# An attention and feed-forward kernel: GpSimd's last block of W_out goes to the second iteration, half of P's low part to GpSimd earlier, its square roots one step later

## What is computed

```python
query = _layernorm(x) @ w_q.T                # 32 heads of 32, in 8 groups of 4
key, value = ctx @ w_k.T, ctx @ w_v.T        # one head of 32 for each group
scores = where(mask, query . key / sqrt(32), lowest)
attention = softmax(scores)
x = x + (attention @ value) @ w_out.T
x1, x2 = split(_layernorm(x) @ w12.T + b12)
x = x + (silu(x1) * x2) @ w3.T + b3
```

## Time and profile before

| | |
|---|---|
| median of three runs | 1118.41 us |
| profiled execution: device time | 1119.04 us |
| profiled execution: span of the instructions | 1117.3 us |
| TensorE busy | 1079.1 us (97%) |
| VectorE / ScalarE / GpSimd busy | 571.1 / 425.3 / 392.8 us |
| mean granted TensorE clock | 0.987 |

### The profile page before, as it was taken

One profiled execution on the slowest core, in us unless ns is written; L12 is line 12 of the kernel. 1 busy time (PEld: TensorE's weight loads), 2 busy tenths in 40 slices (PEclk: granted clock), 3 DMA queues, 4 the chain that ended last, 5 costly groups with the idle time before them and its releaser, 6 DMA issues.

```text
span 1117.3 us, 19426 instructions
## 1 busy us (share of the span) xinstructions
PE 1079.1 (97%) x7952; PEld 658.4 (59%) x7952; DVE 571.1 (51%) x1062; ACT 425.3 (38%) x899; POOL 392.8 (35%) x376
## 2 busy tenths in 40 slices
PE   8887999999999989999999999999999999999998
PEld 7776766767768667676655544444444444444443
DVE  6869776776776766577755322631134111431121
ACT  6757555555656455455566520111110111011100
POOL 2769801613315224157686688112000300121000
PEclk8999899999999999999999999999999999999999
DMA  9657597996988858569793644370006300360001
GB/s 367 213 145 169 134 255 191 204 230 165 251 195 213 208 173 210 121 172 232 183 243 81 175 160 159 71 241 1 1 4 151 147 1 1 76 188 1 1 1 76
DMA packets 201512, 162.24 MB, mean 145 GB/s; under 512 B 162640, under 2 KB 172880, under 8 KB 196560
## 3 DMA queue, kind: packets, MB, share of 16 engines
q1 hardware_dynamic: 201424, 161.01, 54.3%
HBM read 93.87 MB, written 27.26 MB: 108 GB/s over the span
## 4 chain that ended last, share of the span: by engine, by line
PE 75%; DVE 11%; ACT 4%; DMA 2%; issue 1%; POOL 1%; SPq 0%; DVEq 0%; ACTq 0%
PE bank_dense L984 69%; ACT arena_attn L816 2%; DVE arena_in L1356 2%; DMA arena_attn<-arena_attn 2%; PE bank_score L1045 1%; PE bank_score L1041 1%; DVE arena_rows L1328 1%; DVE arena_in L1359 1%; DVE arena_in L1269 1%; DVE arena_rows L1317 1%; PE bank_dense L1001 1%; PE bank_av L1063 1%; PE bank_av L1067 1%; DVE arena_in L1373 1%; PE bank_av L1065 1%
## 5 line engine op out<-in xcount | busy, mean ns | idle before, releaser
L984 PE MATMUL bank_dense<-arena_rows,arena_in 128*128 128x256 f16 (+1 forms) x2304 | 348.1, 309 | 3.6 <-DVE small L1231 1.4
L984 PEld LDWEIGHTS bank_dense<-arena_rows,arena_in 128*128 128x128 f16 x2304 | 224.3, 98 | 111.3 <-DVE small L1231 1.7
L816 ACT ACTIVATE arena_attn<-bank_score,arena_in 128x128 f32<-128x128 f32 x512 | 192.9, 467 | 160.6 <-DVE arena_in L1359 160.6
L984 PE MATMUL bank_dense<-arena_out,arena_attn 128*128 128x512 f16 x768 | 170.5, 379 | 0.0
L984 PE MATMUL bank_dense<-arena_out,arena_in 128*128 128x512 f16 x768 | 166.1, 379 | 0.9 <-issue 0.9
L984 PE MATMUL bank_dense<-arena_attn,arena_rows 128*128 128x512 f16 x768 | 166.4, 379 | 0.0
L1408 DVE SCALAR_TENSOR_TENSOR arena_attn<-bank_dense,small,arena_attn 128x512 f32<-128x512 f32 x32 | 24.0, 751 | 221.3 <-PE bank_dense L984 221.3
L702 POOL TENSOR_TENSOR arena_attn<-arena_attn 128x512 f16<-128x512 f32 x53 | 62.6, 1181 | 199.3 <-ACT arena_attn L825 199.3
L984 PEld LDWEIGHTS bank_dense<-arena_out,arena_in 128*128 128x128 f16 x768 | 75.1, 98 | 91.7 <-issue 1.5
L984 PEld LDWEIGHTS bank_dense<-arena_attn,arena_rows 128*128 128x128 f16 x768 | 75.1, 98 | 90.6
L658 POOL TENSOR_TENSOR small<-small 128x1 f32<-128x1 f32 x32 | 24.1, 755 | 289.7 <-DVE small L1311 289.6
(11 more groups left out here) (124 smaller groups left out, 1326.1 us busy)
## 6 DMA issues: line engine op xcount, KB each, us to landing
arena_rows<-x SPq DMA_DIRECT2D x32, 512.0 KB, 6.0
arena_attn<-q_scratch SPq DMA_DIRECT2D x48, 256.0 KB, 4.6
arena_rows<-w_t SPq DMA_DIRECT2D x12, 1024.0 KB, 6.1
arena_rows<-ctx_t SPq DMA_DIRECT2D x8, 1024.0 KB, 5.9
q_scratch<-arena_attn SPq DMA_DIRECT2D x16, 512.0 KB, 5.2
x_scratch<-arena_rows SPq DMA_DIRECT2D x16, 512.0 KB, 3.9
arena_out<-x_scratch SPq DMA_DIRECT2D x16, 512.0 KB, 6.0
out<-arena_out SPq DMA_DIRECT2D x16, 512.0 KB, 3.8
```

Source lines behind the costliest of these rows:

```text
L816: ins = act.activation(e[:, g % 2, u, SEQ * j:SEQ * j + SEQ], B_SCORE[g % 2][:, SEQ * h:SEQ * h + SEQ], ACT.Exp, bias=neg_max[:, g % 2, h: ...
L984: ins = pe.matmul(dst, lhs(a, c), rhs(b, c), start=(c == 0 and n == 0), stop=(c == KC - 1 and n == 2))
```

## The change

Three things are moved; no arithmetic is added or left out.

- `PLO_ALONE` goes from 11 to 6: for groups 6 to 10 too, GpSimd does the half u = 1 of P's low part and VectorE only the half u = 0.
- GpSimd splits the three blocks of W_out in the steps listed in `WO_AT`. The first two blocks stay in steps (1, 2) to (1, 5). The third (block 1 of W_out) goes from steps (1, 6) and (1, 7) to steps (2, 1) and (2, 2), behind the context's halves.
- The roots of tiles 2t + 2 and 2t + 3, t < 7, go from steps 2 and 3 to steps 3 and 4.

```diff
-PLO_ALONE = 11
+PLO_ALONE = 6
...
+WO_AT = ((1, 2), (1, 3), (1, 4), (1, 5), (2, 1), (2, 2))
...
                         prob_lo(GROUPS * (t - 1) + s - 1)
                     if t < NB and s in (0, 1):
                         split_ctx(t, halves[s])
-                    if t == 1 and s >= 2:
-                        split_wo(s // 2 - 1, WO_ORDER[s // 2 - 1], halves[s % 2])
-                    if t < NB - 1 and s in (2, 3):
-                        root(2 * t + s)
+                    if (t, s) in WO_AT:
+                        n = WO_AT.index((t, s))
+                        split_wo(n // 2, WO_ORDER[n // 2], halves[n % 2])
+                    if t < NB - 1 and s in (3, 4):
+                        root(2 * t + s - 1)
```

## The result

Over 11 runs of each, the changed kernel takes 1125.68 us (1123.10 to 1129.92) and the kernel before 1117.77 us (1109.40 to 1119.38). The medians lie 7.9 us apart. The ratio is 1.0084, with a 95% interval of 1.0064 to 1.0104: slower by 7 to 12 us. A second comparison, beside other kernels, gave 1.0088 (1.0057 to 1.0120). The forecast was +10.0 us and 1128.4 us, with a range of 1123.5 to 1133.0.

A forecast was written before the change was run, and what follows sets the result against it. TensorE, busy 1079.1 of 1117.3 us, was taken to bound the kernel. A projection start 7.5 us later plus 2.5 us of low clock gave +10.0 us, 1128.4 us against the median of 1118.41; range 1123.5 to 1133.0 us.

The forecast's parts named there:

- The queue of GpSimd: Iteration 2: W_out's pieces queue behind context and low parts, so the first output projection starts at 155.5 us, +7.5 us.
- The shift of iteration 1: Everything from 125 us on was to come 2.5 us earlier, with 1 and 6 us as ends.
- The lock: VectorE and GpSimd share a port pair; three meetings at about 0.9 us each would end the block at 156.3 us.
- the five reliefs of 0.53 us: VectorE's operations on P's low part, groups 6 to 10: each shrinks from 1.21 to 0.68 us, 2.65 us in all.
- The low clock: Behind TensorE's wait at the first output projection: lower clock costs 2.5 us, bounds 0 and 3.4.
- The sum: Whole kernel: 7.5 us later projection plus 2.5 us of clock, +10.0 us, with nothing given back behind step (2, 3).
- the signs by which the prediction would have been wrong: Wait under 3 us, shift at 125 us over 6 us, or iterations from 3 on differing by over 1 us each.
- What came along at nothing: Later transposes of P, SyncE's queue, exponentials and roots: covered by the wait or without effect, zero.
- The relief: End of iteration 1: TensorE's 1.79 us wait for VectorE goes, up to 1.6 us of clock returns; shift 2.5 us.
- Faster: Rival: all twelve W_out pieces ready before TensorE at 145.5 us, only the relief left, 1115.4 us; 5%.
- Slower, but less: Rival: short pieces, projection starts at 152.0 us, clock stays, 1122.5 us, or 1124.2 with one short dip; 17%.
- slower, and more: Rival: long pieces and a long clock dip, 11.4 + 3.4 = 14.8 us, 1133.2 us; 16%.

The follow-up runs named there:

- the second trace: The changed kernel unaltered, run and traced once more beside other kernels, against the kernel before: ratio 1.0088 (1.0057 to 1.0120).
- wo_roots: Changed kernel with PLO_ALONE back at 11, W_out's last block in iteration 2 and later roots kept: ratio to the kernel before 1.0015 (0.9996 to 1.0034).
- wo_alone: Kernel before with only W_out's last block moved to steps (2, 1) and (2, 2): ratio 1.0027 (1.0005 to 1.0050).
- clock_kept: Changed kernel with 80 idle transposes on TensorE ahead of its wait for W_out: ratio to the kernel before 1.0072 (1.0044 to 1.0100).
- wo_first: Changed kernel with W_out's last block in steps (2, 0) and (2, 1), ahead of the context's halves: ratio to the kernel before 1.0053 (1.0022 to 1.0084).
- roots_alone: Kernel before with only the roots one step later: ratio 1.0006 (0.9988 to 1.0024).
- plo_alone: Kernel before with only the threshold of P's low part at 6: ratio 1.0007 (0.9985 to 1.0030).
- half_later: Changed kernel with the first half of W_out's last block back in (1, 6), the second in (2, 1): ratio to the kernel before 1.0010 (0.9993 to 1.0027).
- half_roots: Changed kernel with PLO_ALONE back at 11 and W_out's last block in (1, 6) and (2, 1): ratio to the kernel before 0.9999 (0.9989 to 1.0010).
- wo_back: Changed kernel with W_out's last block back in (1, 6) and (1, 7): ratio to the kernel before 0.9972 (0.9957 to 0.9986), repeated 0.9991 (0.9978 to 1.0003).

## Why the prediction was right

**The queue of GpSimd: right, nearly to the microsecond.** Every step of the sum has its row in the first trace. The shift of iteration 1 was taken as 2.5 us; the high part of group 8 was ready at 131.94 + 1.12 = 133.06 us (forecast 133.0). GpSimd idled 1.61 us ahead of its low part (1.6). The four pieces behind it ran from 134.25 to the start of the next low part, 147.13 us: 12.9 us (13.4). The last two took 154.60 - 148.24 = 6.4 us (6.7). TensorE came at 154.71 - 9.22 = 145.49 us (145.5) and started at 154.71 us (155.5). The price of 3.35 us for a piece, from the context pieces of the same iteration, was the right row to choose; they came to 3.2 us. The 3.75 us of iteration 1 would have put the start near 158 us.

**The lock: it sets single pieces, not the sum.** VectorE's timeline:

```profile
114.52 0.23 DVE L1362 TENSOR_SCALAR arena_in<-arena_in 128x8 f32<-128x8 f32 x1
...
115.58 0.67 DVE L1368 TENSOR_TENSOR arena_attn<-arena_attn 128x512 f16<-128x512 f32 x1
...
128.28 1.54 DVE L1368 TENSOR_TENSOR arena_attn<-arena_attn 128x512 f16<-128x512 f32 x1
...
135.23 0.68 DVE L1368 TENSOR_TENSOR arena_attn<-arena_attn 128x512 f16<-128x512 f32 x1
...
151.12 0.68 DVE L1368 TENSOR_TENSOR arena_attn<-arena_attn 128x512 f16<-128x512 f32 x1
```

The small scaling of the earlier trace rows that took 1.09 us takes 0.23 at 114.52 us, now that no split runs beside it, as forecast; the half low part takes 0.67 us at 115.58 us. But the half at 128.28 us took 1.54 us: GpSimd's scaling of 128.23 to 129.27 us began 0.05 us before it. So one of the five reliefs of 0.53 us was no relief. That fits the exclusive lock on the shared port pair (the Trainium skill, SBUF — State Buffer, Reading the diagram under SBUF: two separate sides), in the direction against VectorE. The end of 156.3 us that the prediction drew from the rule was too late, but not for the number of meetings: there were three. The price of 0.9 us came from a meeting with a whole low part of 1.22 us, while VectorE now has halves of 0.68 us. GpSimd's rounding at 135.36 us, begun 0.13 us into the half of 135.23 us, took 1.03 us in place of the 0.61 us of the rounding at 138.80 us; its rounding at 141.89 us took 1.02 us, and its scaling at 151.26 us, 0.14 us into the half of 151.12 us, took 1.44 us in place of 1.04. That is 0.4 us each, and 153.6 + 1.2 = 154.8 us, against 154.60 measured.

**The low clock: right in kind, 0.3 us off in the first trace and 0.9 in the second.** Windows of 2 us over the wait and the projection:

```profile
148.00:150.00 2.00, 0.00 (x0) 0.00 (x0) 1.93 (x6) 0.00 (x0) 1.89 (x3) 1.00 0.23 46
150.00:152.00 2.00, 0.00 (x0) 0.00 (x0) 1.77 (x3) 0.76 (x3) 1.89 (x2) 0.53 1.15 212
152.00:154.00 2.00, 0.00 (x0) 0.00 (x0) 0.00 (x0) 0.75 (x3) 1.86 (x3) 0.50 0.02 4
154.00:156.00 2.00, 1.29 (x4) 0.49 (x5) 0.00 (x0) 0.00 (x0) 2.00 (x3) 0.50 0.00 0
156.00:158.00 2.00, 2.00 (x6) 0.68 (x5) 0.00 (x0) 0.00 (x0) 0.22 (x1) 0.50 0.55 107
158.00:160.00 2.00, 2.00 (x6) 0.73 (x5) 0.00 (x0) 0.00 (x0) 0.00 (x0) 0.50 1.29 209
160.00:162.00 2.00, 2.00 (x9) 0.83 (x8) 0.00 (x0) 0.00 (x0) 0.00 (x0) 0.91 0.80 307
162.00:164.00 2.00, 2.00 (x17) 1.55 (x16) 1.06 (x3) 0.92 (x3) 0.00 (x0) 1.00 1.01 418
```

TensorE is idle in 148 to 154 us and its clock falls within 150 to 152 us; it is at 0.50 until about 160 us. The projection lost 8.12 - 5.35 = 2.8 us (forecast 2.5, bounds 0 and 3.4). In the second trace it lost 1.6 us, and the windows say why. There the clock was at 0.84 in 146 to 148 us, at 0.50 up to 156 us, at 0.60 in 156 to 158 us and at 1.00 from then on. So it fell near 147.4 us, 2.4 us after TensorE stopped, and was back near 157.6 us, 3.3 us into the projection. In the first trace it fell near 150.1 us, 4.6 us after TensorE stopped, and was back near 160.4 us, 5.7 us into the projection. The projection lost half of those stretches at the lower clock: 1.6 of 3.3 us and 2.8 of 5.7 us. Behind a wait of 2.74 us (wo_roots) the projection lost nothing, and behind 3.49 us (wo_alone) 1.4 us. That idling is the cause is shown by clock_kept, in its trace.

**The sum.** In the profiled executions: the stretch grew by 44.03 - 32.55 = 11.5 us, what lies ahead of it shrank by 2.0 us, and what lies behind it, 1117.3 - 157.47 = 959.8 us, took 1128.1 - 166.99 = 961.1 us. That is 11.5 - 2.0 + 1.3 = 10.8 us, against a forecast of 10.0. In the second trace it is 10.4 - 2.4 - 0.7 = 7.2 us. Over all runs it is 0.84%, 9.4 us, with 7.9 us between the medians. So the forecast lies within what the runs spread over; that one trace came within a microsecond of it is in part luck.

Behind the second projection nothing came back, as forecast. The 1.3 us there aren't explained: in the second trace the rest took 1124.5 - 165.40 = 959.1 us, 0.7 us less than before. They arise late. From the second projection to the start of a high part in the last iteration (566.70 us before, 575.50 and 573.84 us in the changed kernel) it is 409.2, 408.5 and 408.4 us, so iterations 3 to 7 as a whole are no longer than before. None of the signs by which the prediction would have been wrong came: the wait is not under 3 us, the shift not over 6, and the later iterations are not each over 1 us longer or shorter.

**What came along at nothing.** The waits of P's transposes in iteration 2 were covered, as forecast, and wo_first shows what they cost when they aren't: 3.96 us. In iteration 3 TensorE waits for a transpose, 1.61 us up to 227.89 us in the first trace and 1.95 us in the second, where the trace of before has no such wait. It isn't of one part of the change: roots_alone, plo_alone and wo_alone have one of 1.8 to 2.0 us there, and wo_roots, half_later and clock_kept have none. The roots cost and gained nothing (roots_alone).

**The relief: a right size by a split that doesn't hold.** The shift at the end of iteration 1 was 2.0 us in one trace and 2.4 in the other, against 2.5 forecast. The forecast hangs on this term one for one, since the start of the projection follows from the high part of group 8. But where the shift comes from differs between the two traces. In the first, the wait of 1.79 us for VectorE shrank to 0.15 us, yet the value projection started only 0.5 us earlier, at 118.72 us; the rest is its length of 2.79 us in place of 4.27. In the second the wait was still 1.52 us, the value projection started 2.6 us earlier, at 116.58 us, and took 4.46 us: the clock fell there again. The prediction had the wait go, for a start 1.2 to 2.2 us earlier, and up to 1.6 us of clock besides; neither trace shows both. wo_alone, without the earlier halves, has the wait of 1.62 us and a shift of 3.3 us. And half_roots, which has a shift of 3.7 us in its trace and no wait for W_out, shows no gain over its runs. That the term came out near 2.5 us is luck as far as these runs tell.

**The rivals.** "Faster" needed pieces of 2.3 us; the fastest here took some 3.0 us, as from 125.21 to 128.23 us. "Slower, but less" and "slower, and more" had the right mechanism and the ends of the prices; neither end came, though the second trace, 7.2 us over before, lies on the side of the former.

## What to carry to other kernels

Before work goes to an in-order queue that has slack, list everything that will stand ahead of the consumer's last piece there, waits on other engines included, and add it up from the latest of those waits. The slack of 25.3 us that the prediction starts from isn't free: the four context pieces stand in it up to 137.01 us, and only 147.96 - 137.01 = 10.95 us are left for a block that takes some 13 us. So the moved block by itself overran it by some 3 us; three small operations of 1.16 us and the waits that come with them, with the low clock behind, turned these 3 us into 9. Edits that are free one by one have to be summed where they share a queue.

A wait of TensorE can cost more than its length, when the clock falls in it, and where the views write "issue" or an engine long done for a wait on several semaphores, the wait is found by putting its end beside the other engines' timelines.

## What the runs showed of the hardware

The low clock behind a wait doesn't cost the same each time: 9.22 and 9.25 us of idling cost 2.8 and 1.6 us behind them, 3.49 us cost 1.4 us, and 2.74 and 1.21 us cost none. In the first two what differed was when the clock fell, 4.6 and 2.4 us after TensorE had stopped. The length of the wait doesn't settle it either: in the kernel before, the low clock of the earlier trace rows in 74 to 78 us stands behind a wait of 1.74 us, and that in 108 to 116 us behind one of 1.98 us and two shorter ones. Eighty transposes without use through the wait (8.90 us) kept the clock at 1.00.

Where GpSimd's operation of 128x512 begins some 0.1 us into a half low part of VectorE (0.68 us), it takes 0.4 us longer; begun 0.14 us into a whole one (1.22 us), it took 0.9 us longer. Begun 0.05 us ahead, it made VectorE's half take 1.54 us.

The end of iteration 1 lies between 119.23 and 126.37 us over the 13 traces of the table. The kernels differ, but two traces of one kernel differ by up to 1.5 us too. It goes loosely with the clock of 62 to 122 us: 0.97 where the point came first (clock_kept) and 0.89 in the trace of before and in the first of wo_back, but 0.91 both in roots_alone, where it came last, and in half_roots (121.24 us). Over whole executions the same shows: of 87 of the kernel before, those with a mean clock of 0.995 took 1114.7 us on average (8 of them), those with 0.989 1119.5 us (12). One trace can't tell a gain of 2 us.
